# Graph layers on one core: 76 hot blocks of far keys in place of 88, the combining of expert outputs shared with ScalarE and TensorE, GpSimd out of the end

## The reference

```python
x = x + gnn(layernorm(x), adj)           # neighbour sum, 128->512, rmsnorm, silu, 512->128
x = x + ffn(layernorm(x), edge_index)    # the layer below

h = (x @ W_gat).reshape(M, 4, 4)                       # heads x experts
e = leaky_relu(a_src[src] + a_dst[dst], 0.2)           # 524288 edges and one loop per node
alpha = softmax of e over the edges with the same dst
agg = segment_sum(h[src] * alpha, dst) + b_gat
scores = layernorm(agg).reshape(.., heads, experts).mean(heads)
g = softmax over the two best scores, zero for the other experts
out = sum over the 4 experts of g[e] * (gelu(x @ W1[e] + b1[e]) @ W2[e] + b2[e])
```

## Time and profile before

| | |
|---|---|
| profiled execution, its span | 1138.47 us, 1136.7 us |
| TensorE matmuls busy | 801.8 us, 71% |
| VectorE busy | 904.1 us, 80% |
| ScalarE busy | 436.9 us, 38% |
| GpSimd busy | 609.0 us, 54% |
| counting loop's matmuls, line 730 | 1232 x, 159.2 us |
| gathers, line 555 | 384 x, 460.8 us |

### The profile page before, as it was taken

The page is one execution under the profiler, slowest core; times in us unless marked ns, Lnnn a source line. Parts: engine busy times, 40 slices in busy tenths (PEclk is TensorE's granted clock), DMA queues, the critical chain, the costliest instruction groups (busy, mean ns, idle before and its releaser), DMA issues. The chain is left out here.

```text
span 1136.7 us, 17715 instructions
## 1 busy us (share of the span) xinstructions
PE 801.8 (71%) x5180; PEld 684.2 (60%) x5180; DVE 904.1 (80%) x3070; ACT 436.9 (38%) x1069; POOL 609.0 (54%) x553
## 2 busy tenths in 40 slices
PE   0003999999999969969999999999995505040130
PEld 0003778878888858848888888888883404040130
DVE  7998899867888859996999303888887488889877
ACT  1008899965555526525555553000001213021203
POOL 2000000027777750377777777888887778787004
PEclk9999788879999969979999998555555555555555
DMA  8000111122222102212222200000000113425001
GB/s 253 4 0 14 38 45 44 33 54 50 49 56 57 18 8 43 78 47 66 84 65 84 83 10 8 7 7 7 7 7 10 43 16 102 139 66 174 19 23 37
DMA packets 73043, 55.45 MB, mean 49 GB/s; under 512 B 32534, under 2 KB 65689, under 8 KB 72988
## 3 DMA queue, kind: packets, MB, share of 16 engines
q1 hardware_dynamic: 56140, 48.72, 13.5%
q0 software_dynamic: 16384, 5.54, 5.4%
q10 hardware_dynamic: 464, 0.59, 0.2%
HBM read 36.65 MB, written 17.76 MB: 48 GB/s over the span
## 5 line engine op out<-in xcount | busy, mean ns | idle before, releaser
L555 POOL DMA_INDIRECT sb_arena<-table,sb_arena x384 | 460.8, 1200 | 169.8 <-issue 116.7
L539 POOL DMA_INDIRECT sb_late<-lists,sb_window_at x128 | 128.1, 1001 | 282.4 <-DMA lists<-sb_arena 240.7
L1314 DVE TENSOR_TENSOR sb_late<-sb_far_lo,sb_iota_lo 128x1792 bf16<-128x1792 bf16 x88 | 96.1, 1092 | 84.0 <-PE ps_four L730 79.5
L730 PE MATMUL ps_four<-sb_late 128*128 128x64 bf16 x1232 | 159.2, 301 | 4.2 <-DVE sb_late L1316 0.3
L730 PEld LDWEIGHTS ps_four<-sb_late 128*128 128x128 bf16 x1232 | 141.8, 143 | 21.4 <-DVE sb_late L1316 18.1
L703 PE MATMUL ps_four<-sb_we,sb_arena 128*128 128x128 f32 x1024 | 131.9, 282 | 0.0
L703 PEld LDWEIGHTS ps_four<-sb_we,sb_arena 128*128 128x128 f32 x1024 | 119.7, 192 | 14.7 <-issue 14.7
L695 PE MATMUL ps_H<-sb_x2nT,sb_we 128*128 (+1 forms) x512 | 124.7, 388 | 0.0
L896 ACT ACTIVATE sb_arena<-ps_H,sb_be_c 128x256 f32<-128x256 f32 x256 | 107.1, 470 | 30.7 <-PE ps_H L695 28.9
L695 PEld LDWEIGHTS ps_H<-sb_x2nT,sb_we 128*128 128x128 f32 x512 | 95.2, 196 | 11.0
L821 ACT ACTIVATE sb_arena<-sb_arena,sb_owner_mid 128x368 f32<-128x368 f32 x128 | 76.9, 601 | 52.7 <-DVE sb_arena L1057 49.8
(11 more groups left out here) (247 smaller groups left out, 1416.9 us busy)
## 6 DMA issues: line engine op xcount, KB each, us to landing
outputs<-sb_arena SPq DMA_DIRECT2D x24, 512.0 KB, 2.6
sb_arena<-outputs SPq DMA_DIRECT2D x12, 1024.0 KB, 6.3
sb_arena<-in_adj SPq DMA_DIRECT2D x32, 256.0 KB
sb_arena<-table,sb_arena POOLq DMA_INDIRECT x384, 2.8
sb_x2nT<-in_L_ffn_edge_index SPq DMA_DIRECT2D x8, 512.0 KB, 7.6
sb_xs<-in_x SPq DMA_DIRECT2D x32, 128.0 KB, 2.2
out_x<-sb_xs SPq DMA_DIRECT2D x16, 256.0 KB, 2.6
sb_late<-lists,sb_window_at POOLq DMA_INDIRECT x128
```

The costliest lines, as they stand in the source:

```text
L539: pool.indirect_dma_start(bk.bitcast(i32)[:, p * WINDOW:(p + 1) * WINDOW], None, lists, bass.IndirectOffsetOnAxis(ap=window_at[:, p:p + 1] ...
L555: pool.indirect_dma_start(rows[:, g, c, o, :], None, table[0:M, :], bass.IndirectOffsetOnAxis(ap=idxT[:, at:at + 1], axis=0), bounds_check ...
L730: last = nc.tensor.matmul(ps_F, hot_lo[k][:, :, c], hot_hi[k][:, :, c], start=(first and c == 0), stop=(end and c == FB - 1))
L1314: V.tensor_tensor(hot_lo[k], far_lo[:, bass.ds(b * FB, FB)].unsqueeze(1).to_broadcast([P, P, FB]), iota_lo[:, :, :], ALU.is_equal)
```

## The change

The far keys. Ranks 6 to 35 of each segment are copied; ranks 0 to 5, with real keys struck out, join ranks 36 to 55 in the row from which the largest are taken, 104 by 13 passes. That fills 76 x 14 = 1064 columns.

The parts. Each bank takes sums of six tiles and not of four, so three banks hold what four held, `take_bank` has four reductions and not two, and two banks (`block_bank`) are free for sums of blocks. Of the four blocks of a part VectorE combines two, one before and one between or behind `take_bank`. The other two are scaled in place by ScalarE (`scale_block`, 16 activations), summed over the experts by four TensorE matmuls with the identity (`block_sum`) and added to the rows by one instruction of VectorE (`add_sum`). In parts 1 and 2 the third block is scaled behind the merge's exponentials and added behind the gates; the fourth block of part 1 is scaled behind the by-head copy of part 2 and added behind `lowest`. In part 3 three blocks (the fourth of part 2 and its own first two) come ahead of all else of that part; VectorE combines its last two.

The end. VectorE combines ten tiles and not eight; six others are gated by ScalarE, summed with their row by five TensorE matmuls and copied back by ScalarE. Stores are of one group (two tiles) and not two.

```diff
-FULL_FAR, REST_FAR, FARCOLS = 36, 72, 88 * FB
+SKIP_FAR, FULL_FAR, REST_FAR, FARCOLS = 6, 36, 104, 76 * FB
+PER_BANK = 6
-KEPT_BLOCKS = 2
+KEPT_TILES = 10
+        marks_bank = [halfH[2], bank_O[:, :]]
+        block_bank = [bank_S[:, :], halfH[3]]
+        SUMMED = (2, 3, 6, 7, 8, 9)
@@ gpsimd @@
-            pool.wait_ge(s["gates_ready"], PARTS)
-            for n, (of, t) in enumerate(others):
-                row = xs[:, t, :]
-                pool.wait_ge(s["gated"], n + 1)
-                pool.tensor_tensor(of[:, 0:2 * D], of[:, 0:2 * D], of[:, 2 * D:4 * D], ALU.add).then_inc(s["sum_chain"], 1)
...
@@ tensor @@
             def mark(g):
-                    pe.wait_ge(s["agg_out"], 2 * g - 1)
+                    pe.wait_ge(s["agg_out"], 2 * g)
...
+            def block_sum(b):
+                pe.wait_ge(s["scaled"], SUMMED.index(b) + 1)
+                some(pe, s["combined"], b - 1, None)
+                of = eo_back[SLOT_OF[b]]
+                for e in range(EXPERTS):
+                    last = nc.tensor.matmul(block_bank[b % 2], ident[:, :], of[:, :, e * D:(e + 1) * D],
+                                            start=(e == 0), stop=(e == EXPERTS - 1))
+                last.then_inc(s["block_in_psum"], 1)
...
             for g in range(PARTS):
+                if g == PARTS - 1:
+                    for b in (block_of(g - 1, 3), block_of(g, 0), block_of(g, 1)):
+                        block_sum(b)
...
+                if g == 2:
+                    block_sum(block_of(g - 1, 3))
...
+                if g in (1, 2):
+                    block_sum(block_of(g, 2))
+            pe.wait_ge(s["agg_out"], 2 * PARTS)
+            for n, (of, t) in enumerate(others):
+                pe.wait_ge(s["gated"], n + 1)
+                for e in range(EXPERTS):
+                    nc.tensor.matmul(others_bank[n], ident[:, :], of[:, e * D:(e + 1) * D], start=(e == 0), stop=False)
+                nc.tensor.matmul(others_bank[n], ident[:, :], xs[:, t, :], start=False, stop=True).then_inc(s["others_in_psum"], 1)
@@ scalar @@
+            def scale_block(b):
+                act.wait_ge(s["gates_ready"], b // PART_BLOCKS + 1)
+                act.wait_ge(eo_loaded[SLOT_OF[b]], 16 * turns(b))
+                for u in range(BLOCK_TILES):
+                    for e in range(EXPERTS):
+                        of = eo_back[SLOT_OF[b]][:, u, e * D:(e + 1) * D]
+                        last = nc.scalar.activation(of, of, ACT.Identity, scale=gates[:, b * BLOCK_TILES + u, e:e + 1])
+                last.then_inc(s["scaled"], 1)
...
+            for g in range(PARTS):
+                if g == PARTS - 1:
+                    for b in (block_of(g - 1, 3), block_of(g, 0), block_of(g, 1)):
+                        scale_block(b)
+                by_heads(g)
+                if g == 2:
+                    scale_block(block_of(g - 1, 3))
...
+                if g in (1, 2):
+                    scale_block(block_of(g, 2))
@@ vector @@
-            V.memset(far_k[:, full_far + REST_FAR:], 0.0)
-            V.tensor_copy(far_k[:, 0:full_far].rearrange("p (g n) -> p g n", g=segments), lev1[:, :, 0:FULL_FAR])
+            V.tensor_copy(far_k[:, 0:full_far].rearrange("p (g n) -> p g n", g=segments), lev1[:, :, SKIP_FAR:FULL_FAR])
+            V.scalar_tensor_tensor(rest[:, 0:first_ranks].rearrange("p (g n) -> p g n", g=segments), lev1[:, :, 0:SKIP_FAR], first_real,
+                                   lev1[:, :, 0:SKIP_FAR], ALU.is_lt, ALU.mult)
...
             for g in range(PARTS):
                 if g == PARTS - 1:
-                    combine(before.pop(0))
-                    combine(before.pop(0))
+                    for b in (block_of(g - 1, 3), block_of(g, 0), block_of(g, 1)):
+                        add_sum(b)
                 weights(g)
...
+                if g == 2:
+                    add_sum(block_of(g - 1, 3))
+                if g:
+                    combine(block_of(g, 0 if g < PARTS - 1 else 2))
                 take_bank(2 * g)
                 take_bank(2 * g + 1)
+                if g:
+                    combine(block_of(g, 1 if g < PARTS - 1 else 3))
                 merge(g)
                 gating(g)
+                if g in (1, 2):
+                    add_sum(block_of(g, 2))
-            for b in range(KEPT_BLOCKS):
-                combine(BLOCKS + b)
+            combine_kept(0, 4)
+            combine_kept(4, 4)
+            combine_kept(8, KEPT_TILES - 8)
```

More of the change, by code:

```diff
@@ L323, in build @@
                  "gates_e", "gates_exp", "gates_ready", "hh_in_psum", "hh_ready", "eo_in_psum", "eo_used",
-                 "combined", "others_combined", "sum_chain", "gated", "iota_done", "zero_done"]
+                 "scaled", "block_in_psum", "combined", "others_combined", "others_in_psum", "gated", "iota_done", "zero_done"]
         s = {n: sem(n) for n in names}
@@ L795, in _ @@
                     for b in range(BATCH):
-                        at = b % 4 * 3 * ROW
+                        at = b % PER_BANK * 3 * ROW
                         for c in range(CHUNKS):
-                            last = nc.tensor.matmul(sums[k % 2][0:OWN, b // 4, at:at + 3 * ROW], hot[k % 2][:, c, :, b],
+                            last = nc.tensor.matmul(sums[k % 2][0:OWN, b // PER_BANK, at:at + 3 * ROW], hot[k % 2][:, c, :, b],
                                                     parts[k % 2][:, c, b, :, :].rearrange("p s v -> p (s v)"),
@@ L1590, in combine @@
                 last.then_inc(s["combined"], 1)
+                gated_n[0] += (EXPERTS - 1) * BLOCK_TILES
             for g in range(PARTS):
-                before = [PART_BLOCKS * (g - 1) + b for b in range(PART_BLOCKS)] if g else []
                 hots_of(2 * g)
@@ L1604, in _, with combine_kept @@
                 lowest(2 * g + 1)
[L1605 to L1606 removed]
+                if g == 2:
+                    add_sum(block_of(g - 1, 3))
+                if g:
+                    combine(block_of(g, 0 if g < PARTS - 1 else 2))
                 take_bank(2 * g)
                 take_bank(2 * g + 1)
[L1609 to L1610 removed]
+                if g:
+                    combine(block_of(g, 1 if g < PARTS - 1 else 3))
                 merge(g)
                 gating(g)
[L1613 to L1614 removed]
+                if g in (1, 2):
+                    add_sum(block_of(g, 2))
+            def combine_kept(first, n):
+                base = gated_n[0] + (EXPERTS - 1) * first
+                for e in range(EXPERTS):
+                    for u in range(n):
+                        row = xs[:, TILES - PAIR * KEPT + first + u, :]
+                        if e:
+                            dve.wait_ge(s["comb_chain"], base + (e - 1) * n + u + 1)
+                        last = V.scalar_tensor_tensor(row, eo_kept[:, first + u, e * D:(e + 1) * D],
+                                                      gates[:, TILES - PAIR * KEPT + first + u, e:e + 1], row, ALU.mult, ALU.add)
+                        if e < EXPERTS - 1:
+                            last.then_inc(s["comb_chain"], 1)
+                        elif u % PAIR:
+                            last.then_inc(s["combined"], 1)
+            combine_kept(0, 4)
+            combine_kept(4, 4)
+            combine_kept(8, KEPT_TILES - 8)
 _INS = ["x", "adj", "L0_gnn_epsilon", "L0_gnn_W1", "L0_gnn_b1", "L0_gnn_rms_weight", "L0_gnn_W2", "L0_gnn_b2",
```

94 lines of the change are left out of this document (53 added, 41 removed).

## The result

The changed kernel takes 1110.36 us (median of 4 runs, 1106.15 to 1111.54), the kernel before 1137.19 (median of 4 runs): a ratio of 0.9749, 95% interval 0.9723 to 0.9775, so 26.8 us less. Predicted were 1109 us and 28.3 less.

What follows compares the result with a forecast made beforehand. Taken as limits: TensorE in the counting loop, VectorE's chain in the parts, GpSimd's gathers close behind. -22.3 + 0.2 - 3.7 - 3.0 + 6.0 + 0.3 - 5.8 = -28.3, giving 1109 us; range 1103 to 1122.

Steps and rivals of the forecast that it cites:

- hot loop: TensorE's counting loop: 12 blocks fewer at 1.857 us each, -22.3 us; VectorE's larger selection hidden in its idle time.
- part 1: Between second reduction and gating: one combined block hides under the 96 KB move, with added reductions and sum, -3.7 us.
- part 2: Like the part before it: 8.4 us becomes 4.5, plus 0.2 for reductions and 0.7 for the added sum, -3.0 us.
- head of part 3: First hot write to weights: three blocks through ScalarE and TensorE come first, 12.0 us becomes 18.0, +6.0 us.
- end: From part 3's gates to the span's end: adds at 0.265 us without GpSimd, last store issued earlier, -5.8 us.
- the sign that the prediction named for being wrong: ScalarE waiting over 5 us for gathered rows or a block's load, or sums of 7 us each.
- T+18: Part 3's weights 18.0 us after T, its first hot write forecast at 1019.9, so at 1037.9 us.
- -6.7 and -11.5: GpSimd's gathers: 6.7 us earlier as twelve leave the loop, 11.5 from shorter hangs; last rows land at 1032.3.
- Rival two: Gathers' hangs beside VectorE's combining do not shrink: last rows at 1043.8, weights 9.2 us late, 1118 us; chance 0.14.
- Rivals one (clock): TensorE stays at 1.2 GHz in part 3's block sums: weights 9 us later than forecast, 1122.5 us; chance 0.14.
- three (load): Third block's load in part 3's head holds up ScalarE; slower than before if it takes 37 us; chance 0.03.
- rival four: A partition needs more than 104 free places, so the slow path over 4160 edge tiles runs, over 20 ms; chance 0.01.

Runs made afterwards that it cites:

- experiment 5: Kernel before with only the selection changed to 76 hot blocks; combining and end as they were: 1129.32 us, ratio 0.9918.
- 6: Changed kernel with the old 88 hot blocks: 1124.66 us, ratio 0.9879 to the kernel before.
- experiment 2: Changed kernel, loads of blocks 10 and 11 issued only after part 3's last gathered rows landed: 1110.41 us, ratio 0.9758 to the kernel before.
- the base: Changed kernel unaltered, timed again as common base of the follow-up runs: 1110.51 us, ratio 0.9768 to the kernel before.
- 7: Changed kernel with VectorE combining all four blocks of a part again; 76 hot blocks and new end stay: 1120.85 us, ratio 0.9848 to the kernel before.
- 9: Changed kernel, loads of blocks 10 and 11 after the last gathered rows, plus three pauses per block in VectorE's combining: 1106.14 us, ratio 0.9721.
- 10: Changed kernel, loads of blocks 10 and 11 after the last gathered rows, plus twelve pauses per block in VectorE's combining: 1108.2 us, ratio 0.9749.
- 11: Kernel before with 76 hot blocks and three pauses per block in VectorE's combining, no block moved, old end: 1120.47 us, ratio 0.9836.
- 12: Changed kernel, loads unaltered, with one pause in the middle of each block VectorE combines in parts 1 and 2: 1105.69 us, ratio 0.9697.
- 3: Changed kernel with a small GpSimd memset at the program's end, behind the last of the other tiles' sums: 1114.73 us, ratio 0.9788.
- 4: Changed kernel with the same small GpSimd memset placed earlier, behind the last gates, as control: 1108.87 us, ratio 0.9749.
- 8: Changed kernel with the old end (VectorE 8 tiles, GpSimd adds 8, stores of four tiles): 1118.11 us, ratio 0.982.

## Why the prediction was right, and where it was not

| step | predicted us | measured us |
|---|---|---|
| hot loop | -22.3 | -22.3 |
| part 0 | +0.2 | -0.1 |
| part 1 | -3.7 | -4.1 |
| part 2 | -3.0 | -3.5 |
| head of part 3 | +6.0 | +11.4 |
| weights to gates, part 3 | +0.3 | +0.5 |
| end | -5.8 | -9.5 |
| sum | -28.3 | -27.6 |

(Measured from row to row as in the prediction; the steps sum to -27.6, loop and tail to -27.5.) The time came out within 2 us because two misses cancelled: the head grew by 5.4 us more than forecast, the end shrank by 3.7 more. That is luck. The loop, parts 0 to 2, the adds at 0.265 us and the clock of the sums in the head came as reasoned.

**Loop.** Right to the tenth: 168 matmuls less at the measured pace. That it stays TensorE's is its row: 135.9 of 141.1 us busy, 1.4 of waiting for VectorE. That the larger selection costs nothing is the row with 52.3 us of waiting. But experiments 5 and 6 say what the term alone doesn't: 9 us of it arrive without the split and 14 to 16 with it, as the gathers don't move with the loop.

**Head of part 3.** The step that failed is the one by which the last rows land at 1032.3, just ahead of ScalarE's asking; the sign that the prediction named for being wrong, over 5 us of waiting for rows, did come. The own work was sized rightly: T+18 forecast, 16.7 and 17.2 measured where rows are in time. Rows came 8.7 us later against T than forecast: 3.7 because the loads of blocks 10 and 11, which the new order issues at T+10.5, stood before the last rows' landing (experiment 2); 2.1 because from the first gather (468.31, before 471.37) to the end of the last the gathers took that much longer than the -6.7 and -11.5 said; 2.9 because T came that much earlier against the first gather (1.7 by the chance in the front, 1.2 by parts that gained more than forecast). Rival two (hangs don't shrink) was wrong by itself: they fell from 19.8 to 9.0 us (10.6 in the base), against 8.3 forecast. Rivals one (clock) and three (load) fell by the rows of the head; rival four fell too, as the slow loop of over 20 ms did not run.

**The hangs' cause.** The prediction weighed the Trainium skill (SBUF — State Buffer, section "SBUF: two separate sides"): VectorE and GpSimd share a port, held for one whole instruction. That GpSimd's issuing of a gather is held off by VectorE's rows of gated adds, experiments 7 and 9 to 12 show; that the port is what does it, no run shows. The length does not fit: by that rule a hang would be 0.27 us at most, one add, and they lasted until the row of adds paused, 6.77 us beside one of 8.48. Nor does every row of instructions with two inputs do it. In the changed kernel two TENSOR_TENSOR of 1.3 us each, both inputs in SBUF, follow each other without a gap, and the gathers beside them pass in 1.00 us:

```profile
921.05 2.64 DVE L1539 TENSOR_TENSOR sb_late<-sb_arena,sb_late 128x1152 bf16<-128x1152 f32 x2
...
921.00 1.00 POOL L566 DMA_INDIRECT sb_arena<-table,sb_arena  x1 [0.30 <-issue]
922.31 1.00 POOL L566 DMA_INDIRECT sb_arena<-table,sb_arena  x1 [0.30 <-issue]
```

**End.** -5.8 was adds without GpSimd beside them and the last store. What failed is the "6.5 us" that "follow" the last store, taken as fixed. The last store was issued 12.15 us after the gates (11.7 forecast), but only 2.3 us followed. 2.9 of the 4.2 us between are GpSimd's drain, shown by experiments 3, 4 and 8; of the rest the smaller last store may be 0.8 (in the profile after, 128 KB land in 1.9 us and 256 KB in 2.7), which wasn't tried; the other 0.5 stays open.

## What to carry to other kernels

A gain in one stage arrives only as far as the other producers of the next stage can keep up: follow the last input of each stage (here gathers issued by GpSimd), not the bounding engine alone. When an indirect transfer's issue stands for several us, look for a row of VectorE instructions without a gap beside it, here SCALAR_TENSOR_TENSOR adds, and put one wait into it before moving work to other engines. If the program's end is tight, give GpSimd nothing in its last 8 us or so: that is what its drain took here.

## What had not been expected of the hardware

- One wait inside 16 adds (4.28 to 4.39 us) removed hangs of 3 to 5 us; for the wait for rows one did as much as three or twelve.
- GpSimd's drain at the program's end took 8.07 us behind a memset of 0.12 us and 8.42 behind adds, VectorE's 0.53 us (changed kernel).
- Two 1 MB loads issued 4 us ahead of the last gather moved its landing from 1.7 to 5.4 us behind its end; the DMA engines' share was 1.0 in 1028 to 1032 us.
